# The order of the ternary product's two jobs on the tensor engine in a fused transformer layer

## What is computed

```python
xn  = layernorm(x)                                   # x: 8 x 2048 x 256
q, k, v = split(xn @ Wqkv + bqkv)
qp, kp  = elu(q) + 1, elu(k) + 1
kv  = einsum('bsd,bse->bde', kp, v)                  # one per batch
attn = einsum('bsd,bde->bse', qp, kv) / (qp . sum(kp) + 1e-6)
z   = layer_norm(xn + attn) * g1 + b1
ffn = (silu(z @ Wg + bg) * (z @ Wu + bu)) @ Wd + bd  # hidden size 682
s   = layer_norm(z + ffn) * g2 + b2
t   = clip(round(weight / scale), -1, 1); scale = mean(|weight|)
out = x + s * silu(xn @ (t * scale).T)               # "the ternary product"
```

## Time and profile before

| | |
|---|---|
| three runs | 1208.73, 1210.75, 1210.92 us; median 1210.75 |
| the profiled execution | 1209.84 us |
| its span, first to last instruction | 1208.1 us |
| PE busy | 1187.2 us (98%) |
| DVE busy | 1079.5 us (89%) |
| ACT busy | 953.2 us (79%) |
| POOL busy | 843.7 us (70%) |
| granted TensorE clock, mean | 0.998 |

### The profile page before, as it was taken

The page is one execution under the profiler, slowest core; times in us unless marked ns, Lnnn a source line. Parts: engine busy times, 40 slices in busy tenths (PEclk is TensorE's granted clock), DMA queues, the critical chain, the costliest instruction groups (busy, mean ns, idle before and its releaser), DMA issues.

```text
span 1208.1 us, 24021 instructions
## 1 busy us (share of the span) xinstructions
PE 1187.2 (98%) x7550; PEld 1067.3 (88%) x7550; DVE 1079.5 (89%) x2467; ACT 953.2 (79%) x1557; POOL 843.7 (70%) x994
## 2 busy tenths in 40 slices
PE   8999999999999999999999999999999999999997
PEld 6889998989988999988989989899988999888886
DVE  6988999999999999999999999999999999777765
ACT  7787888878888888888878888788887878867753
POOL 3443787767787776787757887677886767766676
PEclk9999999999999999999999999999999999999999
DMA  7213432334432334432334432244332343222201
GB/s 216 78 48 88 123 106 70 88 106 123 123 104 72 88 106 123 122 105 73 88 106 122 110 103 83 75 123 123 109 96 67 97 123 105 71 71 63 76 21 36
DMA packets 137523, 115.61 MB, mean 96 GB/s; under 512 B 12339, under 2 KB 122293, under 8 KB 137398
## 3 DMA queue, kind: packets, MB, share of 16 engines
q1 hardware_dynamic: 137398, 114.08, 32.6%
HBM read 67.38 MB, written 46.67 MB: 94 GB/s over the span
## 4 chain that ended last, share of the span: by engine, by line
PE 52%; DVE 21%; ACT 11%; issue 9%; DMA 3%; POOL 2%; SPq 1%; DVEq 0%; ACTq 0%; POOLq 0%
PE bank L1271 36%; PE d_bank L1271 11%; PE xk_bank L1271 5%; DVE st L922 3%; DVE bank L1095 3%; ACT rz L695 3%; DVE rz L1054 2%; DVE h_l L1105 2%; DMA xa<-z_turned 2%; DMA z_turned<-xa 2%; ACT h_h L695 1%; DVE zT_l L1085 1%; ACT ku L695 1%; POOL norm L569 1%; ACT hs L695 1%
## 5 line engine op out<-in xcount | busy, mean ns | idle before, releaser
L1271 PE MATMUL bank<-zT_h,wgu_h 128*128 128x512 f32 x704 | 275.1, 391 | 1.1 <-DVE rz L1054 1.1
L1271 PE MATMUL bank<-zT_l,wgu_h 128*128 128x512 f32 x704 | 275.1, 391 | 0.0
L1271 PE MATMUL bank<-zT_h,wgu_l 128*128 128x512 f32 x704 | 275.0, 391 | 0.0
L695 ACT ACTIVATE rz<-rz,norm 128x256 f32<-128x256 f32 x252 | 140.5, 595 | 53.6 <-DVE norm L1131 53.6
L569 POOL TENSOR_TENSOR norm<-ve,consts 128x4 f32<-128x4 f32 x64 | 72.9, 1139 | 154.7 <-DVE ve L933 154.5
L1271 PE MATMUL d_bank<-wd_h,h_h 128*128 128x256 f32 x640 | 179.4, 280 | 0.1
L1271 PE MATMUL d_bank<-wd_h,h_l 128*128 128x256 f32 x640 | 179.2, 280 | 0.0
L1271 PE MATMUL d_bank<-wd_l,h_h 128*128 128x256 f32 x640 | 179.2, 280 | 0.0
L1095 DVE SCALAR_TENSOR_TENSOR bank<-bank,hb,hs 128x512 f32<-128x512 f32 x160 | 117.9, 754 | 53.6 <-ACT hs L695 41.9
L695 ACT ACTIVATE h_h<-bank 128x512 fp32r<-128x512 f32 x160 | 95.7, 598 | 80.7 <-DVE bank L1095 80.4
L1271 PEld LDWEIGHTS bank<-zT_l,wgu_h 128*128 128x128 f32 x704 | 132.2, 188 | 28.1
(11 more groups left out here) (163 smaller groups left out, 3571.8 us busy)
## 6 DMA issues: line engine op xcount, KB each, us to landing
xq<-in_L_attn_x_dram SPq DMA_DIRECT2D x32, 512.0 KB, 5.9
xa<-in_L_attn_x_dram SPq DMA_DIRECT2D x31, 512.0 KB, 3.9
out_dram<-rz SPq DMA_DIRECT2D x31, 512.0 KB, 5.0
z_turned<-xa SPq DMA_DIRECT2D x120, 128.0 KB, 3.3
xa<-z_turned SPq DMA_DIRECT2D x30, 512.0 KB, 4.1
turned<-xa SPq DMA_DIRECT2D x108, 128.0 KB, 2.4
xa<-turned SPq DMA_DIRECT2D x27, 512.0 KB, 3.9
rz<-in_L_attn_Wg_dram SPq DMA_DIRECT2D x1, 640.0 KB, 5.7
```

Of the source, the lines that this page charges most:

```text
L695: return eng.activation(out_, in_, func, **kw).then_inc(S[name], 1)
L1271: ins = eng.matmul(dst, left, right, start=first and n == 0, stop=last and n == len(pairs) - 1, **kw)
```

## The change

The ternary jobs keep their size and number and get new places in TensorE's list. B 0 goes from the place ahead of U 2 to the place where B 1 stood, ahead of G 3. B 1 goes from there to the place between U 4 and XK 1. On ScalarE, `silu_tern 0` goes from the place behind `h_high 1` to the place where `silu_tern 1` stood, and `silu_tern 1` goes to the place between `h_high 3` and `x_high 1`. VectorE's, GpSimd's and SP's lists are the same, and so are the lists of the fill and the end.

```diff
 TENSOR_JOBS = steps("""
-    K 0, D 4, KV 0, KV 1, D 5, K 1, N 0, N 1, N 2, N 3, G 0, U 0, G 1, U 1, G 2, B 0, U 2, Q 0, Q 1,
-    B 1, G 3, D 0, D 1, U 3, G 4, XK 0, U 4, XK 1, XK 2, XK 3, GU 5, D 2, TZ 0, TZ 1, D 3""")
+    K 0, D 4, KV 0, KV 1, D 5, K 1, N 0, N 1, N 2, N 3, G 0, U 0, G 1, U 1, G 2, U 2, Q 0, Q 1,
+    B 0, G 3, D 0, D 1, U 3, G 4, XK 0, U 4, B 1, XK 1, XK 2, XK 3, GU 5, D 2, TZ 0, TZ 1, D 3""")
 SCALAR_STEPS = steps("""
...
-    last_rows 0, silu_gate 0, h_high 0, silu_gate 1, last_rows 1, h_high 1, silu_tern 0, last_rows 2,
...
-    z_rows 3, q_exp 1, k_high 1, q_high 0, silu_tern 1, q_high 1, silu_gate 3, silu_gate 4, x_high 0,
-    h_high 3, x_high 1, h_high 4, silu_gate 5, xn_high 0, xn_high 1, h_high 5""")
...
+    k_high 1, q_high 0, silu_tern 0, q_high 1, silu_gate 3, silu_gate 4, x_high 0, h_high 3, silu_tern
+    1, x_high 1, h_high 4, silu_gate 5, xn_high 0, xn_high 1, h_high 5""")
```

More of the change, by code:

```diff
@@ L90 @@
 TENSOR_JOBS = steps("""
-    K 0, D 4, KV 0, KV 1, D 5, K 1, N 0, N 1, N 2, N 3, G 0, U 0, G 1, U 1, G 2, B 0, U 2, Q 0, Q 1,
-    B 1, G 3, D 0, D 1, U 3, G 4, XK 0, U 4, XK 1, XK 2, XK 3, GU 5, D 2, TZ 0, TZ 1, D 3""")
+    K 0, D 4, KV 0, KV 1, D 5, K 1, N 0, N 1, N 2, N 3, G 0, U 0, G 1, U 1, G 2, U 2, Q 0, Q 1,
+    B 0, G 3, D 0, D 1, U 3, G 4, XK 0, U 4, B 1, XK 1, XK 2, XK 3, GU 5, D 2, TZ 0, TZ 1, D 3""")
 SCALAR_STEPS = steps("""
     xk_copy 0, zT_high 0, zT_high 1, x_res 0, x_res 1, kv_high 0, kv_high 1, x_res 2, x_res 3, k_exp 0,
-    last_rows 0, silu_gate 0, h_high 0, silu_gate 1, last_rows 1, h_high 1, silu_tern 0, last_rows 2,
-    silu_gate 2, last_rows 3, k_exp 1, k_high 0, q_exp 0, h_high 2, z_rows 0, z_rows 1, z_rows 2,
-    z_rows 3, q_exp 1, k_high 1, q_high 0, silu_tern 1, q_high 1, silu_gate 3, silu_gate 4, x_high 0,
-    h_high 3, x_high 1, h_high 4, silu_gate 5, xn_high 0, xn_high 1, h_high 5""")
+    last_rows 0, silu_gate 0, h_high 0, silu_gate 1, last_rows 1, h_high 1, last_rows 2, silu_gate 2,
+    last_rows 3, k_exp 1, k_high 0, q_exp 0, h_high 2, z_rows 0, z_rows 1, z_rows 2, z_rows 3, q_exp 1,
+    k_high 1, q_high 0, silu_tern 0, q_high 1, silu_gate 3, silu_gate 4, x_high 0, h_high 3, silu_tern
+    1, x_high 1, h_high 4, silu_gate 5, xn_high 0, xn_high 1, h_high 5""")
 VECTOR_STEPS = steps("""
```

## The result

The changed kernel takes 1216.99 us (median of 4 runs, 1215.83 to 1219.19), and beside it, on the same chip, the kernel before takes 1209.82 (4 runs, 1208.73 to 1210.92). The ratio is 1.0066, with an interval of 1.0053 to 1.0079: slower by 0.7%, about 7 us. The forecast was 1221.9 us with a range of 1215 to 1229. Direction and the wait of B 1 came out as forecast; the size was about 5 us too large, 0.9 of it because the forecast started from a median of 1210.75.

The account below looks back on a forecast made before the run. TensorE, busy 98%, was taken to bound a balanced kernel tied at GU 5. Terms 13.8 - 2.1 - 0.6 = +11.1 us on 1209.84 gave 1220.9; plus 0.9 for the median, 1221.9 us, range 1215 to 1229.

Parts of the forecast that it names:

- What bounds the kernel: TensorE busy 98% of the span, without gaps at 35.67 us per iteration (38.07 with KV); engines balanced.
- the tie at GU 5: ScalarE and VectorE tied to TensorE once per iteration; their work from there fills nearly the whole 35.67 us.
- (a): TensorE's B 1 waits for ScalarE's silu_tern 0 to free its bank: 0.39 us late, 0.07 restart, 0.46 us per iteration.
- (b): TensorE's G 4 waits for VectorE's q_elu 0: 0.60 us per iteration with restart; may be absent if k_low 0 precedes last_gate.
- The wait passed on in full: Through GU 5 the wait returns in iterations 1 to 26, TensorE's own work unchanged: 26 x 0.53 = 13.8 us.
- What is won: Time regained: 2.1 us of steady-part disturbances (bounds 0 and 4.1), 0.6 us of the late stall (bounds 0 and 1.1).
- The disturbances: Irregular delays in the steady part before the change, 4.1 us in all; half, 2.1 us, was to vanish.
- The late stall: TensorE idle 0.91 us at 1122.03 behind a transfer of z after ScalarE's z_rows; 0.6 us was to go.
- The signs that were named: Profile: K 0 periods about 36.2 and 38.6 us, brackets at G 4 or B 1, VectorE's h_rows 3 wait 0.6.
- Slip once: Rival: slack of half a microsecond at GU 5, so TensorE shifts only once; 1206.2 us, chance 0.07.
- no wait at all: Rival: VectorE's run from h_rows 5 to h_rows 1 shortens by 0.4 us or more; 1209 to 1211, chance 0.09.
- Contention gets worse: Rival: one more VectorE step slows by 0.53 us in each of 26 iterations; 13.8 us more, 1235.7 us, chance 0.06.

Follow-up runs that it names:

- experiment 1: Changed kernel with ScalarE's q_high 1 put ahead of silu_tern 0, so silu_tern 0 comes later: 1232.11 us, ratio 1.0193 to the kernel before.
- experiment 2: Changed kernel with B 1 moved behind attention sum XK 1 on TensorE: 1212.16 us, ratio 1.0028 to the kernel before.
- experiment 7: Changed kernel with silu_tern 0 ahead of q_high 0 on ScalarE and q_low 0 behind k_low 1 on VectorE: 1210.25 us, ratio 1.0005 to the kernel before.
- experiment 8: Kernel before with B 0 right ahead of B 1 at B 1's old place, silu_tern 0 right ahead of silu_tern 1: 1331.7 us, ratio 1.1011.
- experiment 5: Changed kernel with VectorE's h_low 2 put ahead of k_max 1: 1229.60 us, ratio 1.0174 to the kernel before.
- experiment 6: Changed kernel with h_low 2 ahead of k_max 1 on VectorE and XK 1 ahead of B 1 on TensorE: 1229.12 us, ratio 1.0168.
- experiment 4: Kernel before with only B 1 and silu_tern 1 moved to their new places, B 0 and silu_tern 0 staying: 1206.77 us, ratio 0.9985.

## Why the prediction was right, and where its size was off

**What bounds the kernel, and the tie at GU 5.** Right. Both lists of waits, and experiment 1, where 0.52 us of delay became 0.53 us per iteration, show the loop directly.

**(a) B 1 waits for silu_tern 0.** Right in place. It was put at 0.39 us of lateness and 0.07 of restart, 0.46 in all. In the iteration shown B 1 is 0.27 late (0.50 - 0.23), its eight matmuls take 723.80 - 722.77 = 1.03 instead of 0.94, and U 3 had lost 0.13 before it: 0.49. The prediction left out the wait of U 3 for h_low 2, a term that it put at nothing without a word. What is lost at U 3 doesn't come on top of the wait at B 1: where U 3 was 0.92 and 0.69 us late, B 1 didn't wait at all, and with the 0.13 us of this iteration B 1's lateness would be 0.40, against the 0.39 forecast. The term therefore didn't spoil the sum, but it decided what was left when the wait at B 1 was taken away: a wait of 0.36 to 0.38 us with its restart, and 0.13 to 0.15 us of period in experiments 2 and 7, about 3.5 us of the kernel.

**(b) G 4 waits for q_elu 0.** Absent, and by the row that the prediction named: k_low 0 took 0.68 us. It was the first term that was mis-sized. The prediction took the middle between 0.46 and 0.60, 0.53; with (a) alone it would have been 0.46, and the period grew by 0.39.

**The wait passed on in full.** The prediction took TensorE's own work to be "as long as ever", so that the period grows by what is waited. It isn't quite so long. Of the 0.49 us some 0.07 come back behind B 1: the 18 attention sums and the first five matmuls of GU 5 take 726.99 - 723.80 = 3.19 us where before they took 538.78 - 535.52 = 3.26. In the iteration from 105.44 the two waits with their restarts come to 0.72 us, and its period is 36.10. Without what it waited TensorE's iteration is 36.04 - 0.49 = 35.55 us in the one shown, 35.38 in that one and 35.82 - 0.38 = 35.44 in experiment 2, against 35.67 before, where it waited for nothing. In experiment 8 nothing came back: 38.97 - 35.67 = 3.30 us is the whole wait with its restart. Why the matmuls start closer together in the one kernel than in the other, I don't know. In 26 iterations the loss is 26 x 0.39 + 6 x 0.04 = 10.4 us, against 13.8 forecast for 26 at 0.53.

**What is won.** Forecast 2.1 and 0.6. The disturbances up to the last K 0 are 917.66 - (25 x 36.06 + 6 x 2.44) = 1.5 us instead of 4.1, so 2.6 are won; 0.5 of it is that the one iteration of 35.60 lies below 36.06. From the last K 0 to the end of the span it is 1214.1 - 1023.10 = 191.0 us instead of 192.5, though iteration 26 with its 0.39 lies in this stretch: 1.9 won. The late stall of 0.91 us at 1122.03 is gone from PE's list altogether, which with its restart is about 1.2 us of that and a little more than the bound of 1.1; the other 0.7 I can't place. Together 4.5 instead of 2.7.

**The sum.** 10.4 - 2.6 - 1.9 = +5.9, and the profiled executions differ by 1215.83 - 1209.84 = 6.0; the medians differ by 7.2. Of the 5.2 us between +11.1 and +5.9, 3.4 are the period and 1.8 the part that is won.

**The signs that were named.** The periods are 36.06 and 38.50, for 36.2 and 38.6. The bracket at B 1 stands on the weight load and not on a matmul; there it comes 24 times. VectorE's wait ahead of h_rows 5 came, with 0.42 us for about 0.6. That ahead of h_rows 3 went to 1.33, not 0.6: the forecast subtracted ScalarE's 0.57 us, but k_low 0 had become 0.5 us shorter, and VectorE waited for as much longer. silu_gate 5 starts 0.04 us behind GU 5.

**The rivals.** "Slip once" falls with experiment 1, "no wait at all" with the rows of B 1. "Contention gets worse" didn't come in the changed kernel, where k_max 1 takes 1.30 us in two of the 25 iterations, against three before, and k_low 0 became faster; but it is real: experiments 5 and 6 walked into it, by 13 us, with an edit that I had expected to help.

## What to carry to other kernels

Where result banks go round in the order of the jobs, moving a job changes the releaser of every job up to a ring's length behind it: write down for each moved job whose reader frees its bank, and compare with when that reader ends. In a kernel whose engines are tied to each other once per iteration, a delay on the loop is paid in each round: 0.52 us more of it made each iteration 0.53 us longer. A wait that the timeline shows is not its price, though: 0.15 us at Q 1 cost nothing, 0.38 us at U 3 cost 0.15, so read the period beside it. And the same job can be harmless, or cost 0.7% or 10%, a few places apart. The durations of steps of VectorE and GpSimd that read SBUF belong to an order, and change with it.

## What the runs showed of the chip

**A wait of no length still delays the next matmul.** At U 3 (717.58 in the changed kernel) the matmul was 0.02 us late, and the next followed after 0.34 us instead of 0.23. A semaphore that is released at the very moment it is needed holds the stream up by 0.11 us here. Whether the iteration gets longer by it is another matter: at Q 1 in experiment 4 it didn't.

**The clock behind a long wait.** In experiment 8 the granted clock fell in most iterations behind the wait of 3.03 us. The columns are the stretch, then the busy time and count of PE, PEld, DVE, ACT and POOL, the granted clock, and DMA (its share, and GB/s):

```profile
325.00:332.00 7.00, 7.00 (x40) 6.06 (x39) 6.85 (x24) 6.32 (x11) 5.72 (x8) 1.00 0.00 0
336.00:338.50 2.50, 2.50 (x10) 2.11 (x9) 2.36 (x3) 2.47 (x5) 2.50 (x4) 0.51 0.55 129
```

It was 1.00 ahead of the wait and 0.51 behind it, the level of 1.2 GHz, and matmuls of 512 columns started 0.42 us apart (336.24 to 336.66) instead of 0.23. It was back at 1.00 by 340 us, so that some 3 us of work went at half the pace. That is the 1.5 us by which most iterations exceed 38.97, and about 30 us of the kernel, which my expectation for that run lacked. A wait of the same 3.03 us at 255.90, in an iteration of 38.97, left the clock at 1.00:

```profile
256.00:258.50 2.50, 2.50 (x16) 2.24 (x17) 2.50 (x4) 2.47 (x6) 2.50 (x4) 1.00 0.73 164
```

Why the clock fell in the one and not in the other stays open. The waits of up to 1.4 us in experiments 5 and 6 left the mean clock at 0.997 and 0.998.
